# Turning the normalised keys on TensorE instead of through VectorE and DRAM in a Perceiver block

## The reference

```python
qh = _layernorm((q @ Wq.T).reshape(B, Lq, H, D).transpose(0, 2, 1, 3), gq, bq) * scale
kh = _layernorm((k @ Wk.T).reshape(B, Lk, H, D).transpose(0, 2, 1, 3), gk, bk)
vh = (v @ Wv.T).reshape(B, Lk, H, D).transpose(0, 2, 1, 3)
attn = jax.nn.sigmoid(jnp.einsum('bhqd,bhkd->bhqk', qh, kh))
x = jnp.einsum('bhqk,bhkd->bhqd', attn, vh)
return x.transpose(0, 2, 1, 3).reshape(B, Lq, C) @ Wp.T + bp
```

## Time and profile before

| | before |
|---|---|
| median of three runs | 2916.39 us |
| the profiled execution's own time | 2916.39 us |
| its span | 2914.7 us |
| TensorE busy with matmuls | 2831.7 us, 97% |
| VectorE busy | 1466.7 us, 50% |
| ScalarE busy | 1464.8 us, 50% |
| GpSimd busy | 891.6 us, 31% |
| mean granted clock of TensorE | 0.988 |

### The profile page before, as it was taken

The page is one execution under the profiler, slowest core; times in us unless marked ns, Lnnn a source line. Parts: engine busy times, 40 slices in busy tenths (PEclk is TensorE's granted clock), DMA queues, the critical chain, the costliest instruction groups (busy, mean ns, idle before and its releaser), DMA issues.

```text
span 2914.7 us, 68560 instructions
## 1 busy us (share of the span) xinstructions
PE 2831.7 (97%) x27730; PEld 2271.9 (78%) x27730; DVE 1466.7 (50%) x2158; ACT 1464.8 (50%) x1450; POOL 891.6 (31%) x615
## 2 busy tenths in 40 slices
PE   4999999999999999999999999977999999999999
PEld 3777777777777777777777777736999998999998
DVE  5444444444444444444444444447577765667754
ACT  0555555555545555555555555523546565646554
POOL 2444444444444444444444444410000000000000
PEclk8999999999999999999999999988999999999999
DMA  5333233333333332233333333212545555545453
GB/s 209 84 86 86 80 83 86 82 81 85 86 82 81 85 86 80 83 86 86 80 82 86 83 81 84 76 37 87 180 169 193 181 188 192 199 174 202 179 189 131
DMA packets 194480, 334.46 MB, mean 115 GB/s; under 512 B 21736, under 2 KB 122344, under 8 KB 173040
## 3 DMA queue, kind: packets, MB, share of 16 engines
q1 hardware_dynamic: 194416, 333.56, 36.7%
HBM read 281.57 MB, written 51.90 MB: 114 GB/s over the span
## 4 chain that ended last, share of the span: by engine, by line
PE 80%; DVE 6%; issue 4%; DMA 4%; POOL 4%; SPq 1%; ACT 1%; DVEq 0%; POOLq 0%; ACTq 0%
PE kv_ps L1091 30%; PE f_ps L1330 23%; PE s_ps L1116 10%; PE o_ps L1128 9%; PE y_ps L1314 5%; POOL k_var L462 2%; DMA k_rows<-k_dram 2%; DMA k_dram<-k_blocks 2%; DVE k_n L737 1%; POOL ctx_lo L452 1%; SPq L383 1%; PE pm L1197 1%; DVE w_lo L668 1%; DVE k_blocks L741 1%; DVE v_sb L726 1%
## 5 line engine op out<-in xcount | busy, mean ns | idle before, releaser
L518 ACT ACTIVATE even_probs<-s_ps 128x2048 f32<-128x2048 f32 x196 | 369.0, 1883 | 506.6 <-PE o_ps L1128 344.4
L462 POOL TENSOR_TENSOR k_var<-k_var,neg_half 128x16 f32<-128x16 f32 x196 | 579.7, 2958 | 15.4 <-POOL k_var L458 0.2
L518 ACT ACTIVATE odd_probs<-s_ps 128x2048 f32<-128x2048 f32 x196 | 369.8, 1887 | 193.8 <-PE s_ps L1116 193.8
L668 DVE TENSOR_TENSOR w_lo<-w_raw,w_hi 128x2048 fp32r<-128x2048 f32 x160 | 366.5, 2292 | 173.4 <-ACT w_hi L558 173.3
L452 POOL TENSOR_TENSOR ctx_lo<-ctx_raw,ctx_hi 128x512 fp32r<-128x512 f32 x196 | 252.9, 1290 | 599.3 <-DVE ctx_hi L711 599.3
L1330 PE MATMUL f_ps<-h_hi,w_hi 128*128 128x256 f32 x1536 | 429.1, 279 | 0.0
L1330 PE MATMUL f_ps<-h_lo,w_hi 128*128 128x256 f32 x1536 | 428.1, 279 | 0.0
L1330 PE MATMUL f_ps<-h_hi,w_lo 128*128 128x256 f32 x1536 | 428.1, 279 | 0.0
L730 DVE TENSOR_REDUCE k_var<-k_sq 128x16 f32<-128x512 f32 x196 | 134.5, 686 | 508.3 <-ACT k_sq L524 508.3
L558 ACT ACTIVATE w_hi<-w_raw 128x2048 fp32r<-128x2048 f32 x160 | 305.8, 1913 | 73.3 <-PE y_ps L1314 62.4
L1091 PE MATMUL kv_ps<-wk_hi,ctx_hi 128*128 128x512 f32 x784 | 329.2, 420 | 4.3 <-DVE q_lo L797 2.8
(11 more groups left out here) (196 smaller groups left out, 5031.3 us busy)
## 6 DMA issues: line engine op xcount, KB each, us to landing
w_raw<-w_dram SPq DMA_DIRECT2D x160, 1024.0 KB, 4.8
ctx_raw<-ctx_dram SPq DMA_DIRECT2D x196, 256.0 KB, 2.7
k_dram<-k_blocks SPq DMA_DIRECT2D x784, 64.0 KB, 1.7
k_rows<-k_dram SPq DMA_DIRECT2D x196, 256.0 KB, 2.9
qkv_w<-qkv_w_dram SPq DMA_DIRECT2D x1, 3072.0 KB, 13.8
bias_rows<-bias_rows_dram SPq DMA_DIRECT2D x1, 1280.0 KB, 16.5
wq<-wq_dram SPq DMA_DIRECT2D x1, 1024.0 KB, 5.5
wk_rows<-wk_dram SPq DMA_DIRECT2D x1, 1024.0 KB, 7.6
```

What stands on the lines that cost most here:

```text
L462: g.tensor_tensor(k_var[:, 2], k_var[:, 1], neg_half[:].to_broadcast([P, H]), ALU.pow)\
L518: s.activation(probs[r % 2][half][:], s_ps[:], ACT.Sigmoid).then_inc(probs_made, 1)
L668: v.tensor_tensor(w_lo[i][:], w_raw[i % RAW][:], w_hi[i][:].bitcast(f32), ALU.subtract)\
```

## The change

The way of the keys from `k_n` to `kt_hi` and `kt_lo` is another one. TensorE turns `k_n` with four transposes of 128x128 (`turn_keys`) into the bank of `kv_ps` that is free at that point: bank 0 for an odd tile, bank 1 for an even one (`turned_in`). VectorE splits the result from there (`split_turned`). The 32x32 transpose on VectorE, the DRAM buffer, `k_blocks`, `k_rows` and the five DMAs of each tile go.

```diff
+        def turned_in(r):
+            return kv_ps[:, 1 - r % 2]
...
             with sp.Fori(1, NKT // 4) as it:
                 for r in range(4):
-                    put_keys(it, r - 4)
                     load_ctx(it, r)
-                    get_keys(it, r - 4)
...
+            def split_turned(it, r):
+                dve.wait_ge(t_made, n_of(it, r, 1, 1))
                 wait(dve, s_made, n_of(it, r, 2, -2))
+                turned = turned_in(r).rearrange("p (g k) -> p g k", g=NG)
+                hi, lo = kt_hi[r % 2][:], kt_lo[r % 2][:]
+                v.tensor_copy(hi, turned).then_inc(kt_hi_made, 1)
                 dve.wait_ge(kt_hi_made, n_of(it, r, 1, 1))
+                v.tensor_tensor(lo, turned, hi.bitcast(f32), ALU.subtract).then_inc(kt_lo_made, 1)
...
-                wait(dve, k_blocked, n_of(it, r))
+                wait(dve, t_made, n_of(it, r))
...
-                v.transpose(k_blocks[r % 2][:].rearrange("p q (g k) -> p q g k", g=NG),
-                            k_n[:].rearrange("p (g q) d -> p q g d", g=NG)).then_inc(k_blocked, 1)
...
             def two_tiles(it, r):        # VectorE
+                normalise(it, r - 1)
                 high_part(it, r + 1)
                 sum_squares(it, r)
-                split_keys(it, r - 1)
+                split_turned(it, r - 1)
                 normalise(it, r)
                 copy_values(it, r)
+                split_turned(it, r)
                 high_part(it, r + 2)
                 sum_squares(it, r + 1)
-                split_keys(it, r)
-                normalise(it, r + 1)
                 copy_values(it, r + 1)
...
                     if m == 0:           # projection, TensorE
                         pe.wait_ge(ctx_lo_made, n_of(it, r, 1, 1))
                         wait(pe, k_kept, n_of(it, r))
+                        if r % 2:
+                            wait(pe, kt_lo_made, n_of(it, r, 1, -1))
                     if m == 12:
                         wait(pe, v_copied, n_of(it, r))
+                        if r % 2:
+                            wait(pe, kt_lo_made, n_of(it, r))
...
+            def turn_keys(it, r, last=False):
+                pe.wait_ge(k_normed, n_of(it, r, 1, 1))
+                if r % 2:
+                    pe.wait_ge(k_kept, n_of(it, r, 1, 1 if last else 2))
+                else:
+                    pe.wait_ge(v_copied, n_of(it, r, 1, 1))
+                for grp in range(NG):
+                    ins = t.transpose(turned_in(r)[:, grp * P:(grp + 1) * P],
+                                      k_n[:, HG * grp:HG * grp + HG].rearrange("p h d -> p (h d)"), ident[:])
+                ins.then_inc(t_made, 1)
...
                 projection(it, r, 0, 24) # two_tiles, TensorE
+                turn_keys(it, r - 1)
                 scores(it, r - 2, 0)
...
                 scores(it, r - 2, 1)
+                turn_keys(it, r)
                 projection(it, r + 1, 0, 12)
```

More of the change, by code:

```diff
@@ L137, in perceiver_block @@
         early_probs = [sb(f"even_probs{i}", [P, HG, 2, TOK], f32, first_slots) for i in range(2)]
-        k_blocks = [sb(f"k_blocks{i}", [P, HG, C // HG], f32, first_slots) for i in range(2)]
-        k_rows = [sb(f"k_rows{i}", [P, HG, C // HG], f32, first_slots) for i in range(2)]
         first_slots.close()
@@ L251, in perceiver_block @@
         q_turned_in = s_ps[:, 0:2].rearrange("p a b t -> p (a b) t")
-        k_dram = [nc.dram_tensor(f"k_dram{i}", (P, HG, C // HG), f32).ap() for i in range(2)]
         raw_in = [sem(f"raw_in{i}") for i in range(4)]
@@ L261, in perceiver_block @@
         k_normed = sem("k_normed")
-        k_blocked = sem("k_blocked")
-        k_put = [sem(f"k_put{i}") for i in range(2)]
-        k_moved = [sem(f"k_moved{i}") for i in range(2)]
+        t_made = sem("t_made")
         kt_hi_made, kt_lo_made = sem("kt_hi_made"), sem("kt_lo_made")
@@ L292, in n_of @@
             return it * (4 * per) + (per * r + more)
-        def moved(it, r, per=1):
-            more = 16 * per * (r // 2 + 1)
-            return 32 * per * it + more if isinstance(it, int) else it * (32 * per) + more
+        def turned_in(r):
+            return kv_ps[:, 1 - r % 2]
         def is_first(it, r, t):
@@ L377, in _ @@
                 sp.dma_start(dst[:], a[name]).then_inc(once(name + "_in"), 16)
[L379 to L390, removed]
             with sp.Fori(1, NKT // 4) as it:
                 for r in range(4):
-                    put_keys(it, r - 4)
                     load_ctx(it, r)
-                    get_keys(it, r - 4)
-            for r in range(4):
-                put_keys(NKT // 4 - 1, r)
-                get_keys(NKT // 4 - 1, r)
             with sp.Fori(1, HALVES * CHUNKS_HALF // RAW) as it:
@@ L711, in high_part @@
                 v.tensor_copy(ctx_hi[r % 2][:], raw[r % 4][:]).then_inc(ctx_hi_made, 1)
-            def split_keys(it, r):
-                dve.wait_ge(k_moved[r % 2], moved(it, r))
+            def split_turned(it, r):
+                dve.wait_ge(t_made, n_of(it, r, 1, 1))
                 wait(dve, s_made, n_of(it, r, 2, -2))
-                hi, lo = (k[r % 2][:].rearrange("p g (b k) -> p b g k", b=HG) for k in (kt_hi, kt_lo))
-                rows_ = k_rows[r % 2][:].rearrange("p b (g k) -> p b g k", g=NG)
-                v.tensor_copy(hi, rows_).then_inc(kt_hi_made, 1)
+                turned = turned_in(r).rearrange("p (g k) -> p g k", g=NG)
+                hi, lo = kt_hi[r % 2][:], kt_lo[r % 2][:]
+                v.tensor_copy(hi, turned).then_inc(kt_hi_made, 1)
                 dve.wait_ge(kt_hi_made, n_of(it, r, 1, 1))
-                v.tensor_tensor(lo, rows_, hi.bitcast(f32), ALU.subtract).then_inc(kt_lo_made, 1)
+                v.tensor_tensor(lo, turned, hi.bitcast(f32), ALU.subtract).then_inc(kt_lo_made, 1)
             def copy_values(it, r):
@@ L735, in normalise @@
                 dve.wait_ge(k_dev_made, n_of(it, r, 1, 1))
-                wait(dve, k_blocked, n_of(it, r))
+                wait(dve, t_made, n_of(it, r))
                 v.tensor_tensor(k_n[:, :, 0:D - 1], k_c[:, :, 0:D - 1], per_row(k_var[:, 2], D - 1), ALU.mult)\
                     .then_inc(k_normed, 1)
-                dve.wait_ge(k_normed, n_of(it, r, 1, 1))
-                wait(dve, kt_lo_made, n_of(it, r, 1, -1))
-                v.transpose(k_blocks[r % 2][:].rearrange("p q (g k) -> p q g k", g=NG),
-                            k_n[:].rearrange("p (g q) d -> p q g d", g=NG)).then_inc(k_blocked, 1)
             def two_tiles(it, r):
+                normalise(it, r - 1)
                 high_part(it, r + 1)
                 sum_squares(it, r)
-                split_keys(it, r - 1)
+                split_turned(it, r - 1)
                 normalise(it, r)
                 copy_values(it, r)
+                split_turned(it, r)
                 high_part(it, r + 2)
                 sum_squares(it, r + 1)
-                split_keys(it, r)
-                normalise(it, r + 1)
                 copy_values(it, r + 1)
@@ L800, in _ @@
             copy_values(0, 0)
+            split_turned(0, 0)
             high_part(0, 2)
             sum_squares(0, 1)
-            split_keys(0, 0)
-            normalise(0, 1)
             copy_values(0, 1)
@@ L811, in _ @@
             two_tiles(nq - 1, 6)
-            split_keys(nq, 3)
+            normalise(nq, 3)
+            split_turned(nq, 3)
             dve.wait_ge(av_made, 2 * (NKT + 1))
@@ L1163, in _ @@
             pe.sem_inc(w_used, 2)
+            turn_keys(0, 0)
             projection(0, 1, 0, 24)
@@ L1168, in _ @@
                 two_tiles(it, 6)
+            turn_keys(nq, 3, last=True)
             scores(nq, 2, 0)
```

## The result

The changed kernel takes 2984.88 us, the median of 4 runs (2983.63 to 2998.73), against 2915.35 us for the kernel before (4 runs, 2913.76 to 2920.44). The ratio is 1.0246 with a 95% interval of 1.0213 to 1.0280. It is slower by 2.5%. The forecast was 2992 us. The stated range, 2980 to 3020, held the result; the narrower one of the forecast's own terms, 2986 to 3006, missed it by 1 us.

The account below looks back on a forecast made before the run. TensorE's gapless stream was taken to bound the steady stage: span 2914.7 + 87.9 for turns - 10.3 at the start - 1.7 at the end = 2990.6, with 1.7 around it 2992 us; range 2980 to 3020.

Parts of the forecast that it names:

- The price of a turn: Four transposes per tile on TensorE, steady stage: 0.46 us forecast, bounds 0.44 and 0.52; 87.9 us for 191 turns.
- The switch: Between transposes and the projection's matmuls behind them on TensorE: 0.09 us more, charged to every second turn.
- The new waits: TensorE's waits for VectorE before turns and projections in the steady pair: no cost, slacks of 1.5 to 2.4 us.
- the timetable of the pair: Clock of the new two-tile pair, from the projection of tile r, placing TensorE's and VectorE's work: 19.76 us.
- The start: Up to the first scores: TensorE's 10.08 us idle time goes, scores at 65.6; gain 10.3 us, two turns included.
- The end: After the last pair: TensorE waits for the last k_n, nothing at half clock; gain 1.7 us, three turns included.
- Drained turns: Rival: each turn drains TensorE on both sides, 0.62 us a turn, 3023 us; chance 0.10.
- A wait of the new ring: Rival: late k_n stalls TensorE at a turn; one microsecond beyond the slacks per pair gives 3090 us; chance 0.06.
- The clock: Rival: a tenth of the tiles' stage runs at half clock, 3110 us; chance 0.03.
- No effect: Rival: the change doesn't do what it says, scores' order or DMAs staying the bound, about 2916 us; chance 0.02.
- Transposes one by one: Rival: each of 784 transposes costs TensorE its full 0.272 us, 3117 us; chance 0.03.
- The other side: Rival: transposes fit into TensorE's existing gaps, only the two ends count, 2904 us, 0.4% faster; chance 0.04.

Follow-up runs that it names:

- experiment 5: Changed kernel with the five DMAs of each tile put back, from a constant tile through DRAM to a tile nobody reads: 2987.31 us, ratio 1.0248.
- Experiment 3: Changed kernel with the even tile's turn moved behind the next tile's key projection: 3067.64 us, ratio 1.0529.
- experiment 1: Changed kernel without its 784 transposes, waits and VectorE's new order kept: 2898.71 us, ratio 0.9939 to the kernel before.
- Experiment 7: Changed kernel with GpSimd's addition of the bias to x held until the last keys are split: 2987.12 us, ratio 1.0239.
- experiment 8: Kernel before with the wp and qkv_w loads behind the last keys and GpSimd's bias addition held: 2903.73 us, ratio 0.9957.

## Why the prediction was right

**What bounds the kernel.** Right. The stage of the tiles is TensorE's stream with nothing between, at clock 1.00, and what was added to it came out in full: 0, 4 and 8 transposes for a turn give pairs of 18.84, 19.68 and 20.56 us.

**The removed DMAs are worth 0.** Right in the steady stage, by experiment 5.

**The price of a turn.** This is the term that was mis-sized: 0.46 us forecast, 0.423 measured (81.7 / 193), 0.037 x 191 = 7.1 us too much. The distance of 0.11 us between transposes, from the earlier trace rows, was exact. The switch was not: I charged part of the 0.09 us that the experts' second matmul behind two small transposes is late. I had read those rows on one side only. From the first transpose at 2192.91 to that second matmul at 2193.24 pass 0.33 us for two transposes and one matmul, three steps of 0.11, so the rows charge nothing. What stood in the switch's place is a rebate: scores and projections already pay for a step between them, and a turn in between costs less than its four distances. On the timeline of the kernel before the first projection matmul behind scores takes 0.50 us and the next starts 0.34 later, where 0.23 is usual:

```profile
1892.25 0.50 PE L1091 MATMUL kv_ps<-wv_hi,ctx_hi 128*128 128x512 f32 x1
...
1892.59 0.40 PE L1091 MATMUL kv_ps<-wv_hi,ctx_lo 128*128 128x512 f32 x1
...
1892.82 0.40 PE L1091 MATMUL kv_ps<-wv_lo,ctx_hi 128*128 128x512 f32 x1
```

That the turn takes this step over is my reading of it. Experiment 3 agrees, where the turn is gone from behind the scores and the key projection takes 2.99 us again instead of 2.77. My own lower bound of 0.44 was already above what was measured.

**The new waits cost nothing.** Right, by experiment 1, and the timetable of the pair that it rested on is supported by experiment 3: moved by 2.8 us, the turn makes TensorE wait 0.79 where 0.6 to 0.8 was worked out.

**The start.** 10.3 us forecast, 9.9 measured. Half clock lasted to about 57 instead of 55.5, which takes a part of it. How long it lasts is not fixed by the kernel: in experiments 5 and 7, whose TensorE list is the same up to there, it ended at about 54.6 and 55.2.

**The end.** From the end of the pairs on I had forecast 17.4 us and it was 19.55. I had TensorE stand for 2.8 us and run on at full clock; it stood for 2.73, and the clock fell to 0.64 for the next 4.8. It is a place where I did not carry over to the new idle time what the earlier trace rows show behind the old one. With the last two turns of the loop, 0.85 us, the end takes 20.4 us where it took 20.0: it loses 0.4 us where I had forecast a gain of 1.7. Experiment 7 takes most of the idle time away, and the half clock goes with it.

**The number.** The forecast span was 2990.6 us, the profiled one 2985.2. The turns were 7.1 us too high and the blocks behind came out 0.8 us shorter; the start was 0.4 and the end 2.1 us too favourable. So the errors partly cancelled, 7.1 + 0.8 - 0.4 - 2.1 = 5.4 us, and that is luck. The median lies another 2 us below the profiled execution.

**The rivals.** Drained turns: no, the pieces beside a turn keep their lengths or, behind scores, get shorter. A wait of the new ring: no, TensorE has matmuls for all of the 1775 us. The clock: no, it is 1.00 there. No effect: no, the DMAs are gone and the transposes are there, at 2985 us. Transposes one by one: no; their duration is 0.27 us and their distance 0.11. So the figure of the Trainium skill ("TensorE: Matmul & The Clock Gate", Part 4: PE-mode transpose) agrees as a duration and would have been wrong as a price. The other side: no; 2904 us was what the ends alone would give, and experiment 1, where the turns are left out and so cost nothing, ran at 2899.

## What to carry to other kernels

When one engine's chain has no gap, moving a task onto it costs the whole task, however long the detour that it replaces; a transfer with five DMAs for a tile that nobody on the chain waits for is cheaper than 0.42 us of the bound engine. Price an added instruction by the distance between instructions of its kind in a run of them, not by its duration. And before a detour is torn out because its first trip is slow, look at what else is in the DMA queue at that time: here the order of two loads held the gain of the start, and the kernel before with only that order changed is 2.7% faster than the changed kernel.

## What the runs showed of the hardware

- Two neighbours on VectorE and GpSimd: the last `k_n` takes 2.75 us while GpSimd adds 1024 columns (2.34 us), and 0.68 where that addition is held back (experiments 7 and 8).
- A plain fp32 product with a 128-column identity appears as two matmuls, the transpose as one; in the stream they cost 0.22 and 0.11 us (pairs of 20.62 and 19.68 us, against 18.84 with neither).
- The same idle time can leave the clock at 1.00 or not. Behind 2.08 us before the second scores it stayed at 1.00 in the changed kernel (66 to 74 us); in experiments 5 and 7, whose TensorE list is the same up to there, it was 0.57 behind 2.08 and 2.07 us (68 to 72 and 68.3 to 72 us). What decides it no run here shows.
